# Adjacency rows stored once per two groups, in two transfers of 112 and 13 partitions, from a ring of eight groups' sums

## What is computed

```
scores = jnp.sum(q[dst] * k[src], axis=-1) * scale
scores = scores + (edge_weight[:, None] @ we + be)[:, 0]
seg_max = jax.ops.segment_max(scores, dst, num_segments=n)
exp_s = jnp.exp(scores - seg_max[dst])
denom = jax.ops.segment_sum(exp_s, dst, num_segments=n)
attn = exp_s / jnp.maximum(denom[dst], 1e-12)
message = v[src] * attn[:, None]
out = jax.ops.segment_sum(message, dst, num_segments=n)
```

## Time and profile before

| | us |
|---|---|
| median of 3 runs | 1706.06 (1702.39 to 1709.83) |
| the profiled execution | 1710.91 |
| its span, first to last instruction | 1709.2 |
| adjacency stage on DVE, first sum to last | 143.1 to 801.3 |
| busy share in the span: PE, DVE, ACT, POOL | 90%, 63%, 54%, 43% |

### The profile page before, as it was taken

The page is one execution under the profiler, slowest core; times in us unless marked ns, Lnnn a source line. Parts: engine busy times, 40 slices in busy tenths (PEclk is TensorE's granted clock), DMA queues, the critical chain, the costliest instruction groups (busy, mean ns, idle before and its releaser), DMA issues.

```text
span 1709.2 us, 41008 instructions
## 1 busy us (share of the span) xinstructions
PE 1529.8 (90%) x9767; PEld 1325.5 (78%) x9862; DVE 1079.6 (63%) x2995; ACT 928.7 (54%) x2928; POOL 735.0 (43%) x1149
## 2 busy tenths in 40 slices
PE   6978998999999999998799999999999979974887
PEld 5967888888888888887688888888888869962444
DVE  6725887778877877777455555545555557985221
ACT  4738888888888888887233333333333324530111
POOL 0046777777777777775011111011111005752554
PEclk9989999999999999999899999999999998986897
DMA  8252333333333333334521111222111130124663
GB/s 189 51 163 76 104 101 99 102 101 103 102 102 100 102 101 103 102 101 140 119 81 71 69 70 74 81 81 78 71 67 71 71 75 25 60 67 117 186 181 87
DMA packets 215819, 164.28 MB, mean 96 GB/s; under 512 B 41023, under 2 KB 207884, under 8 KB 212547
## 3 DMA queue, kind: packets, MB, share of 16 engines
q1 hardware_dynamic: 184826, 96.77, 20.9%
q0 software_dynamic: 16544, 57.40, 9.5%
q10 hardware_dynamic: 14400, 9.55, 2.0%
HBM read 82.33 MB, written 85.50 MB: 98 GB/s over the span
## 4 chain that ended last, share of the span: by engine, by line
PE 58%; DMA 15%; DVE 10%; issue 8%; SPq 3%; another core or an unknown queue 2%; ACT 2%; DVEq 1%; POOL 1%; ACTq 0%; POOLq 0%
PE bank L1522 16%; PE bank L1510 13%; DMA adj<-arena 12%; PE bank L1489 8%; DVE arena L1152 4%; PE bank L1529 3%; PE bank L1554 3%; DVE arena L1126 3%; PE bank L1410 3%; PE bank L1562 2%; SPq L522 1%; DMA arena<-rows_dram,arena 1%; PE bank L1473 1%; PE bank L1415 1%
## 5 line engine op out<-in xcount | busy, mean ns | idle before, releaser
L1489 PE MATMUL bank<-arena 128*125 128x128 f32 x4096 | 581.5, 278 | 55.4 <-DVE arena L1126 48.0
L1489 PEld LDWEIGHTS bank<-arena 128*125 128x125 f32 x4096 | 546.5, 187 | 102.6 <-issue 45.6
L829 ACT ACTIVATE arena<-bank,tables 128x128 f32<-128x128 f32 x2048 | 569.6, 375 | 87.4 <-PE bank L1473 58.3
L663 POOL TENSOR_SCALAR arena<-iota_row,held 128x125 f32<-128x125 f32 x768 | 476.8, 635 | 172.7 <-PE bank L1489 165.6
L1152 DVE SCALAR_TENSOR_TENSOR arena<-arena,tables,bank 125x128 f32<-125x128 f32 x1023 | 351.3, 343 | 135.6 <-DMA adj<-arena 76.9
L1522 PE MATMUL bank<-V,arena 125*125 125x256 f32 x1250 | 297.2, 383 | 5.9 <-ACT arena L855 5.9
L855 ACT COPY arena<-bank 125x500 f32<-125x500 f32 (+1 forms) x175 | 90.7, 533 | 379.9 <-PE bank L1529 379.9
L1126 DVE TENSOR_TENSOR arena<-iota_row,tables 128x250 f32<-128x250 f32 x640 | 273.6, 428 | 9.0 <-issue 8.8
L1522 PEld LDWEIGHTS bank<-V,arena 125*125 125x125 f32 x1250 | 223.9, 189 | 38.5 <-ACT arena L855 10.6
L683 POOL COPY gidx<-arow 125x1 uint32 (+1 forms) x25 | 37.5, 1499 | 459.2 <-DVE wk_sb L1193 459.2
L1193 DVE CUSTOM_DVE_ANT_0 arena<-arena 125x3200 f32<-125x3200 f32 x25 | 87.3, 3493 | 222.6 <-ACT arena L838 222.6
(11 more groups left out here) (240 smaller groups left out, 1601.0 us busy)
## 6 DMA issues: line engine op xcount, KB each, us to landing
adj<-arena SPq DMA_DIRECT2D x512, 125.0 KB
q_dram<-arena ACTq DMA_DIRECT2D x25, 125.0 KB
wq_sb<-q_dram SPq DMA_DIRECT2D x25, 125.0 KB, 7.9
rows_dram<-tables SPq DMA_DIRECT2D x25, 125.0 KB
rows_dram<-x SPq DMA_DIRECT2D x25, 125.0 KB
arena<-term_rows SPq DMA_DIRECT2D x192, 8.0 KB
V<-in_x SPq DMA_DIRECT2D x5, 560.0 KB
tables<-in_x SPq DMA_DIRECT2D x5, 560.0 KB
```

The source lines that it names most:

```text
L663: ins = nc.gpsimd.tensor_scalar(Xs[:, j % STAGES, k, :], iota_row[:, 0:TILE], held[:, h, c:c + 1], None, ALU.is_equal)
L829: ins = nc.scalar.activation(Ys[:, q, k, :], dist_bank(j)[:, k * LO:(k + 1) * LO], ACT.Relu, scale=nval_tab[:, bass.ds(i, 1)])
L1489: ins = mm(o, Xs[:, j % STAGES, k, :], Ys[:, j % STAGES, k, :], start=(k % SUB == 0), stop=(k % SUB == SUB - 1))
```

## The change

`stage` becomes a ring of eight groups. SP stores only after odd groups, both groups of a pair at once: one transfer of partitions 0 to 111 and one of partitions 112 to 124, each with 4 runs of 512 B per partition. One semaphore stands for each of the four pairs of the ring, and counts both transfers (32). DVE waits for it only at even groups. The number of transfers, their bytes and the size of a run stay the same.

```
-        stage = view(STAGES * GROUP * LO).rearrange("p (s k l) -> p s k l", s=STAGES, k=GROUP)
+        RING = 2 * STAGES
+        stage = view(RING * GROUP * LO).rearrange("p (s k l) -> p s k l", s=RING, k=GROUP)
...
-                sp.wait_ge(sums_ready, g + 1)
-                sp.dma_start(adj_v[:, bass.ds(g * GROUP, GROUP), :],
-                             stage[0:TILE, j % STAGES, :, :]).then_inc(stored[j % STAGES], 16)
+                if j % 2:
+                    r = j % RING - 1
+                    sp.wait_ge(sums_ready, g + 1)
+                    for rows_ in (slice(0, EVEN), slice(EVEN, TILE)):
+                        sp.dma_start(adj_v[rows_, bass.ds((g - 1) * GROUP, 2 * GROUP), :],
+                                     stage[rows_, r:r + 2, :, :].rearrange("p s k l -> p (s k) l")).then_inc(stored[r // 2], 16)
...
-                pool.wait_ge(stored[q], 16 * (last_group // STAGES + 1))
+                pool.wait_ge(stored[q], 32 * (last_group // RING + 1))
...
-                        pool.wait_ge(stored[q], 16 * (NG // STAGES))
+                        pool.wait_ge(stored[q], 32 * (NG // RING))
...
-                q = j % STAGES
+                q, r = j % STAGES, j % RING
...
-                wait_from(dve, stored[q], 16 * ((BODY // STAGES) * i + j // STAGES))
+                if j % 2 == 0:
+                    wait_from(dve, stored[r // 2], 32 * ((BODY // RING) * i + j // RING))
...
-                    prev = stage[0:TILE, q, k - 1, :] if k else stage[0:TILE, (q - 1) % STAGES, GROUP - 1, :]
+                    prev = stage[0:TILE, r, k - 1, :] if k else stage[0:TILE, (r - 1) % RING, GROUP - 1, :]
...
-                        ins = V_.scalar_tensor_tensor(stage[0:TILE, q, k, :], prev,
+                        ins = V_.scalar_tensor_tensor(stage[0:TILE, r, k, :], prev,
```

More of the change, by code:

```diff
@@ L1146, in sums @@
                         dve.wait_ge(sums_ready, g)
-                    prev = stage[0:TILE, q, k - 1, :] if k else stage[0:TILE, (q - 1) % STAGES, GROUP - 1, :]
+                    prev = stage[0:TILE, r, k - 1, :] if k else stage[0:TILE, (r - 1) % RING, GROUP - 1, :]
                     ps = product_bank(j)[0:TILE, k * LO:(k + 1) * LO]
                     if first:
-                        ins = V_.tensor_copy(stage[0:TILE, q, k, :], ps)
+                        ins = V_.tensor_copy(stage[0:TILE, r, k, :], ps)
                     else:
-                        ins = V_.scalar_tensor_tensor(stage[0:TILE, q, k, :], prev,
+                        ins = V_.scalar_tensor_tensor(stage[0:TILE, r, k, :], prev,
                                                       keep_tab[0:TILE, bass.ds(g * GROUP + k, 1)], ps, ALU.mult, ALU.add)
```

## The result

The changed kernel takes 1657.72 us in the median of 4 runs (1654.74 to 1658.96), against 1706.51 us for the kernel before: a ratio of 0.9692, with a 95% interval of 0.9661 to 0.9724. It is faster by 49 us, where 44 were forecast. The profiled execution took 1657.33 us, its span 1655.6.

What follows compares the result with a forecast made beforehand. Stores of 125 partitions on five or six DMA engines were taken to bound the adjacency stage. 43 us there plus 1 in the passage made 44 off 1710.9, 1667; against the median 1662 us, range 1651 to 1681.

Steps and rivals of the forecast that it cites:

- the passage: From the adjacency stage's last sums through POOL's gather to attention: a gain from nothing to 2 us, taken as 1.
- the reasoning by rate alone: Adjacency stage's stores: at DVE's pace they want 109 GB/s, 6 engines' worth of 16, so they stop being a ceiling.
- the landing: A stored pair lands in 3 to 4 us, at most 7.2, under the 7.4 us until it is wanted again.
- What DVE gets back: DVE's waits in the adjacency stage: 26 us for transfers, 10.5 for PE, 5 for odd groups, 41.5; 43 taken.
- the odd groups: DVE's first sums of odd groups lose one semaphore name: 0.04 us, 128 times, from nothing to 5 us; 5 taken.
- PE's delays: DVE's 31.3 us of waits for PE's products: 10.5 us real, to go with DVE's stall.
- PE's own waits for the one-hots: PE's 48.0 us of waits for DVE's one-hots in the adjacency stage: would still be there and cost nothing.
- The ceiling: Stores of 125 partitions run on five or six engines without rest; the stage goes at their 1.285 us per store.
- SP: SP's issuing in the adjacency stage: stores' wait once per pair, loads keep their place; effect nothing.
- The rule against the change: Two transfers to disjoint partition halves bring nothing; taken as it stands, the rate stays at 1706 us (4%).
- Who is next: Adjacency stage after the change: DVE at 1.20 us per group, ahead of PE's 1.09 and ACT's 1.05.

Runs made afterwards that it cites:

- e2: Kernel before, ring of four, each group stored by itself but in two transfers of 112 and 13 partitions: 1708.88 us, ratio 1.0003 to the kernel before.
- e1: Changed kernel with its ring of eight, but every group stored by itself in one transfer of 125 partitions: 1685.61 us, ratio 0.9837 to the kernel before.
- e3: Changed kernel, but each pair stored in one transfer of 125 partitions: 1681.09 us in a single run.
- e5: Kernel before with the three loads of terms spread, one behind each of three stores: 1643.31 us against 1671.64 on that chip, ratio 0.9829.
- e7: Changed kernel with DVE's one-hot moved behind the second sum in six of eight groups: 1615.15 us, ratio 0.9682 to the kernel before.
- e9: Changed kernel run again unchanged, as measure for two later runs on one chip: 1657.28 us, ratio 0.9701 to the kernel before.
- e4: Changed kernel with the cut at partition 124 in place of 112 (124 and 1 partitions): 1942.26 us in one run.
- e8: Changed kernel with a ring of four groups (two pairs): 1655.06 us in a single run, where the kernel before takes 1671.64.
- e12: Changed kernel with the cut at partition 96 in place of 112 (96 and 29 partitions): 1918.08 us in one run.

## Why the prediction was right, and where its reasons were not

**The time** was 1662 and came as 1658; the sign and the place held, and 49 us came where 44 were forecast. Part of this closeness is luck. The stage gave 52.5 us for the forecast 43, and the passage took 4 where it was to give 1. And the reasoning by rate alone would have let the split by itself gain most (the first expectation of e2), where it gained nothing: the ring and the pairing, which the prediction weighed only as room for the landing, turned out to be needed.

**What DVE gets back.** 26 us for the transfers, 10.5 for PE and 5 for the odd groups made 41.5; the idle time fell by 43.4. That PE's delays would go with DVE's was right: 31.3 us fell to 0.8. PE's own waits for the one-hots were to stay and went from 48.0 to 9.6 us, and the last sum came at 748 us and not at 758. The odd groups' wait was worth a little less: places 3 and 7 start at 0.57 and 0.56 us, places 2, 4 and 6 at 0.59, 128 x 0.03 = 4 us. Not forecast were the other 9 us of the stage's 52.5. Of these, 6.4 are one-hots that went from 428 to 418 ns, and 0.9 the sums (351.3 to 350.4 us busy); the rest is not placed. Why they run shorter no run here isolates.

**The ceiling** is the step that failed, though the sum hung on it only in its sign: "the stage goes at their pace: 512 stores in 658 us, one per 1.285 us". The pace of five engines is 1.217 (e1, e3). That the share of 0.35 never moved was no proof: in e1, at the ceiling, it stands at 0.36 with 107 GB/s for 101. In finer slices the rate of the kernel before does move. Here it is in 40 slices from 480 to 520 us:

```profile
GB/s 98 105 93 106 107 109 89 102 106 109 108 105 89 96 108 108 89 98 109 108 109 108 99 84 105 101 95 96 108 96 108 108 108 82 86 105 97 105 102 106
```

It touches 109 again and again, and falls to 82 to 98 between. The kernel before ran 5% under the ceiling, and e5, which moves nothing but the loads, got most of these 5% back.

**SP.** "the loads keep their place and refill a buffer that is wanted eight groups later. Nothing", and this was the other half. Three loads ahead of a store in a ring of four cost 0.42 us at place 2, once in eight groups, 27 us in all, and probably 8 more at place 5; the ring of eight absorbs it (place 2 at 0.59 us with the loads where they were). The prediction had the 1.20 us of the loads in its sum for the landing and did not ask what they do before the change.

**No single part is the gain.** The stage, in us per group: before 1.286; ring of eight alone 1.219; split alone 1.282; ring, pair and split 1.183. The ring takes away the lateness at place 2. The split lifts the five engines' ceiling of 1.217, but doubles the issues, and SP's ceiling is then 1.28 to 1.30. The pair halves them again. Below all three lies DVE's chain.

**The rule against the change** (the Trainium skill, "DMA: Bandwidth & Descriptors", "Rules for kernel authors": two transfers to disjoint partition halves are not worth it) was weighed rightly. Its reason is that both halves already use all 16 engines, which is not the case of 125 partitions: e3 against the changed kernel has 1.216 to 1.183 us per group. By itself the split was indeed worth nothing (e2), for another reason, SP's issues.

**Who is next.** ACT's 1.05 us per group came from the first turn, which is written out. In the loop a group takes 1.09 us without waits (0.265 + 0.25 + 0.25 + 0.325), and PE too needs 1.09; yet e7 stops at 1.168, for a reason not shown. What taking away half of DVE's gap was worth is 0.015 us per group, and not the 0.09 between DVE's 1.18 and these 1.09.

**The passage** was to give 1 us and took 4 (5.3 in e9). Of the 4, 1.8 are the gather's later start against the last sum's end, 2.3 its length.

## What to carry to other kernels

Where a DMA share is flat and no engine is full, look at the partition count of the transfers: in the stage 112 + 13 was worth 17 us against 125 (e3) and 280 us against 124 + 1 (e4). But a flat share is not yet a ceiling; take the waits by place in the period before naming the cause, since a queue's own order (loads issued ahead of a store) makes the same picture, and look at the issuing engine: an issue took 264 ns in the kernel before and 816 ns in e1, where the transfers were the limit. And count the issues: a split that doubles them can put the issuing engine where the DMA engines were.

## What the hardware showed

- A store of 250 KB as 112 and 13 partitions lands in 2.0 us (e8); one of 125 KB as 125 partitions took 3.6 to 4.3 us.
- The small packets beyond those of the loads tell the engines of a store: 4.6 counted for 125 partitions, 29 for 112 and 13, 17.0 for 96 and 29 (e12), 8.0 for 124 and 1 (e4).
- In a loop a store costs SP 0.54 us where nothing holds it back, 0.32 of it the issue itself (e2). The issue alone takes 0.26 us for 125 partitions, and 0.82 us in the median when the transfers hold it back (e1).
- 29 partitions, a prime number, go at the pace of one engine: 1.712 us per group where 35 rows on one engine make 1.704.
- Four identical ACTIVATE of 128x128 take 1.05 us in written-out code and 1.09 us per group in the loop. Most of the difference stands ahead of the group's first one, where ACT has register and semaphore instructions in the loop; that these are the reason is likely and not shown.
